# Summing a state-space scan over its 16 states by accumulating transfers instead of GpSimd adds

## The reference, cut to what matters

```python
x = x + 0.5 * ffn(layernorm(x))          # "FFN 1": 512 -> 1408 -> 512, ternary weights, sigmoid gate
x = x + ssm(layernorm(x))                # the scan
x = x + 0.5 * ffn(layernorm(x))          # "FFN 2", same weights
```

```python
dt = softplus(dt_raw @ W_dt.T + b_dt)    # per token and channel
h[n] = exp(dt * a[n]) * h[n] + dt * b[n] * xln        # over the tokens, for n = 0..15
y = sum over n of h[n] * c[n]
out = y + xln * D_param
```

## Time and profile before

| | us |
|---|---|
| median of 3 runs (lowest, highest) | 925.68 (922.63, 927.62) |
| profiled execution, first to last instruction | 922.9 |
| one chunk, second to seventh | 98.0 to 98.9 |
| DVE busy | 817.9 (89%) |
| PE busy | 681.0 (74%) |
| POOL busy | 591.3 (64%) |
| ACT busy | 566.3 (61%) |

### The profile page before, as it was taken

One profiled execution on the slowest core, in us unless ns is written; L12 is line 12 of the kernel. 1 busy time (PEld: TensorE's weight loads), 2 busy tenths in 40 slices (PEclk: granted clock), 3 DMA queues, 4 the chain that ended last, 5 costly groups with the idle time before them and its releaser, 6 DMA issues. The chain is left out here.

```text
span 922.9 us, 15428 instructions
## 1 busy us (share of the span) xinstructions
PE 681.0 (74%) x5152; PEld 555.8 (60%) x5152; DVE 817.9 (89%) x1113; ACT 566.3 (61%) x1298; POOL 591.3 (64%) x418
## 2 busy tenths in 40 slices
PE   5566595368986888688986898789769894247568
PEld 4455374157865776567764786578557773035457
DVE  4974999899998999899989998999989998989931
ACT  5413565857587667955795768765885587355232
POOL 0370274776678758866777678876887488637502
PEclk7787797669997999889997998799979998559869
DMA  9300000000001000010001000100000000000000
GB/s 365 89 1 24 0 1 23 1 0 2 1 1 47 1 1 1 10 40 1 2 1 47 1 2 1 47 1 1 1 24 1 1 1 2 23 0 1 23 1 24
DMA packets 15009, 18.82 MB, mean 20 GB/s; under 512 B 3664, under 2 KB 12368, under 8 KB 14928
## 3 DMA queue, kind: packets, MB, share of 16 engines
q1 hardware_dynamic: 14928, 17.80, 5.6%
HBM read 13.60 MB, written 4.19 MB: 19 GB/s over the span
## 5 line engine op out<-in xcount | busy, mean ns | idle before, releaser
L344 PE MATMUL work<-x_hi,q 128*128 128x256 f16 x1408 | 338.0, 286 | 38.9 <-DVE hid L831 20.3
L344 PE MATMUL work<-x_lo,q 128*128 128x256 f16 x1408 | 336.7, 285 | 0.0
L1080 POOL TENSOR_TENSOR shared<-shared 128x1024 f32<-128x1024 f32 x120 | 284.5, 2371 | 60.3 <-DVE shared L902 59.9
L892 DVE TENSOR_TENSOR_SCAN shared<-decay,last_state,shared 128x256 f32<-128x256 f32 x448 | 304.4, 729 | 13.8 <-ACT decay L689 7.3
L689 ACT ACTIVATE decay<-shared,a_neg 128x256 f32<-128x256 f32 x512 | 221.1, 468 | 111.9 <-DVE shared L892 107.4
L1064 POOL TENSOR_TENSOR hid_lo<-hid,hid_hi 128x256 f16<-128x256 f32 x176 | 122.0, 707 | 137.9 <-ACT hid_hi L626 137.1
L344 PE MATMUL work<-hid_hi,q 128*128 128x256 f16 x704 | 162.6, 279 | 38.0 <-POOL hid_lo L1064 18.5
L344 PEld LDWEIGHTS work<-x_hi,q 128*128 128x128 f16 x1408 | 144.7, 103 | 71.8 <-DVE hid L831 25.7
L344 PE MATMUL work<-hid_lo,q 128*128 128x256 f16 x704 | 162.9, 279 | 0.0
L344 PEld LDWEIGHTS work<-x_lo,q 128*128 128x128 f16 x1408 | 144.3, 102 | 23.1
L879 DVE TENSOR_TENSOR shared<-shared,bc_row 128x1024 f32<-128x1024 f32 x128 | 154.9, 1210 | 0.3
(11 more groups left out here) (112 smaller groups left out, 788.2 us busy)
## 6 DMA issues: line engine op xcount, KB each, us to landing
x_in<-xT SPq DMA_DIRECT2D x8, 512.0 KB, 4.0
outT<-x SPq DMA_DIRECT2D x7, 512.0 KB, 3.2
shared<-w1T SPq DMA_DIRECT2D x4, 704.0 KB, 7.0
shared<-w2T SPq DMA_DIRECT2D x4, 704.0 KB, 11.5
shared<-w3T SPq DMA_DIRECT2D x3, 768.0 KB, 13.5
shared<-w3T SPq DMA_DIRECT2D x1, 512.0 KB, 15.2
outT<-x SPq DMA_DIRECT2D x2, 256.0 KB, 2.2
wx<-w_xT SPq DMA_DIRECT2D x1, 256.0 KB, 11.4
```

Source lines behind the costliest of these rows:

```text
L344: return nc.tensor.matmul(out, lhsT, rhs, start=start, stop=stop)
L892: nc.vector.tensor_tensor_scan(out=states[:, n % HR, k, :], data0=decay[pair][:, j, :], data1=dbx[:, n % 2, k, :], initial=state, op0=ALU. ...
L1080: nc.gpsimd.tensor_tensor(x2[:, par, :, :] if n == NS - 1 else y[:, 0, :, :], x1d[:, par, :, :] if n == 0 else y[:, 0, :, :], prod[:, n % ...
```

## The change

The sum is made by transfers that add their source to what stands in their destination (`accum_op=ALU.add`), each issued by POOL. The products of the even states go onto `x1d`, which holds the skip path and the residual already. The product of state 1 is written by DVE straight into `y`, and those of the other odd states (3 to 15) are added onto `y`. The ring of products has four tiles instead of two. `sum_up` adds `x1d` and `y` into `x2` on POOL, in step 1 of the next chunk, and `fold_x2` moves from step 0 to step 1 with it. In the last chunk DVE makes that last add, after waiting for the transfers. POOL's chunks are written out one after another instead of in a loop over pairs of them.

```diff
 AT_POOL = dict(
-    ..., fold_x2=1, ...
+    ..., fold_x2=11, sum_up=11, ...
-        prod = carve(2)
+        prod_low = carve(2)
...
+        prod_high = sb("prod_high", [P, 2, KD, TC])
+        prod = [prod_low[:, 0], prod_low[:, 1], prod_high[:, 0], prod_high[:, 1]]
...
@@ ACT, d_times_xln (writes the skip path of chunk c)
-                    act.wait_ge(y_done, NS * (c - 2) + 1)
+                    act.wait_ge(x2_done, c - 1)
@@ DVE, times_c
-                if not (isinstance(g, int) and g < 2):
-                    dve.wait_ge(y_done, g - 1)
-                nc.vector.tensor_tensor(prod[:, n % 2, :, :], states[:, n % HR, :, :], ...
+                if n == 1:
+                    if not first(c):
+                        dve.wait_ge(x2_done, c)
+                elif n % 2 == 0 and not (isinstance(g, int) and g < 4):
+                    dve.wait_ge(even_added, 16 * (NS // 2 * c + n // 2 - 1))
+                elif n % 2 == 1 and not (isinstance(g, int) and g < 7):
+                    dve.wait_ge(odd_added, 16 * ((NS // 2 - 1) * c + max(0, n - 5) // 2))
+                nc.vector.tensor_tensor(y[:, 0, :, :] if n == 1 else prod[n % 4], states[:, n % HR, :, :], ...
@@ DVE, after the last chunk
-            dve.wait_ge(y_done, NS * NC - 1)
-            dve.wait_ge(prod_done, NS * NC)
-            nc.vector.tensor_tensor(x2[...], y[:, 0, :, :], prod[:, (NS - 1) % 2, :, :], ALU.add).then_inc(y_done, 1)
+            dve.wait_ge(even_added, 16 * (NS // 2) * NC)
+            dve.wait_ge(odd_added, 16 * (NS // 2 - 1) * NC)
+            nc.vector.tensor_tensor(x2[...], y[:, 0, :, :], x1d[:, (NC - 1) % 2, :, :], ALU.add).then_inc(x2_done, 1)
@@ POOL
-            def add_y(c, n, par):
...
-                nc.gpsimd.tensor_tensor(x2[:, par, :, :] if n == NS - 1 else y[:, 0, :, :],
-                                        x1d[:, par, :, :] if n == 0 else y[:, 0, :, :],
-                                        prod[:, n % 2, :, :], ALU.add).then_inc(y_done, 1)
+            def add_prod(c, n, par):
+
+                if n % 2 == 0:
+                    count = NS // 2 * c + n // 2
+                    if n == 0:
+                        pool.wait_ge(x1d_done, c + 1)
+                    else:
+                        pool.wait_ge(even_added, 16 * count)
+                    pool.wait_ge(prod_done, NS * c + n + 1)
+                    nc.gpsimd.dma_start(x1d[:, par, :, :], prod[n % 4], accum_op=ALU.add).then_inc(even_added, 16)
+                elif n > 1:
+                    count = (NS // 2 - 1) * c + n // 2 - 1
+                    if n > 3:
+                        pool.wait_ge(odd_added, 16 * count)
+                    pool.wait_ge(prod_done, NS * c + n + 1)
+                    nc.gpsimd.dma_start(y[:, 0, :, :], prod[n % 4], accum_op=ALU.add).then_inc(odd_added, 16)
+
+            def sum_up(c, par):
+
+                pool.wait_ge(x2_free[par], 8 * (c - par) + 16)
+                pool.wait_ge(even_added, 16 * (NS // 2) * (c + 1))
+                pool.wait_ge(odd_added, 16 * (NS // 2 - 1) * (c + 1))
+                nc.gpsimd.tensor_tensor(x2[:, par, :, :], x1d[:, par, :, :], y[:, 0, :, :], ALU.add).then_inc(x2_done, 1)
@@ POOL, beside_scan(c, par, now)
+                    if now == AT_POOL["sum_up"]:
+                        sum_up(c - 1, 1 - par)
                     if now == AT_POOL["fold_x2"]:
-                        pool.wait_ge(y_done, NS * c)
+                        pool.wait_ge(x2_done, c)
                         fold(pool, nc.gpsimd, fold_x[2], c, square[2], x2[:, 1 - par, :, :])
@@ POOL, scan_chunk
                     if s > 0:
-                        add_y(c, s - 1, par)
+                        add_prod(c, s - 1, par)
                     elif not first(c):
-                        add_y(c - 1, NS - 1, 1 - par)
+                        add_prod(c - 1, NS - 1, 1 - par)
...
-            scan_all(pool, scan_chunk)
+            for c in range(NC):
+                scan_chunk(c, c % 2)
+            add_prod(NC - 1, NS - 1, (NC - 1) % 2)
```

More of the change, by code:

```diff
@@ L65 @@
     lo1=[10, 11, 11, 21, 30, 30, 30, 40, 40, 40, 40],
-    lo2=[70, 71, 81, 90, 101, 110, 120, 120, 121, 121, 121], fold_x2=1, fold_sq2=30, x_lo2=41, softplus=140,
+    lo2=[70, 71, 81, 90, 101, 110, 120, 120, 121, 121, 121], fold_x2=11, sum_up=11, fold_sq2=30, x_lo2=41, softplus=140,
     fold_x0=60, x_lo0=141, bc_rest=120, add_x1=91)
@@ L201, in macaron @@
         dbx_done, scan_done = sem("dbx_done"), sem("scan_done")
-        prod_done, y_done = sem("prod_done"), sem("y_done")
+        prod_done, x2_done = sem("prod_done"), sem("x2_done")
+        even_added, odd_added = sem("even_prods_added"), sem("odd_prods_added")
         state_saved = sem("state_saved")
@@ L899, in times_c @@
                 dve.wait_ge(bc_done, g + 3)
-                if not (isinstance(g, int) and g < 2):
-                    dve.wait_ge(y_done, g - 1)
-                nc.vector.tensor_tensor(prod[:, n % 2, :, :], states[:, n % HR, :, :], bcast(bc_row[(n + 1) % 2][:, 1, :]),
+                if n == 1:
[5 more added lines that the diff above has]
+                    dve.wait_ge(odd_added, 16 * ((NS // 2 - 1) * c + max(0, n - 5) // 2))
+                nc.vector.tensor_tensor(y[:, 0, :, :] if n == 1 else prod[n % 4], states[:, n % HR, :, :], bcast(bc_row[(n + 1) % 2][:, 1, :]),
                                         ALU.mult).then_inc(prod_done, 1)
@@ L1034, in _ @@
             dve.wait_ge(x2_free[(NC - 1) % 2], 8 * (NC - 2) + 16)
-            dve.wait_ge(y_done, NS * NC - 1)
-            dve.wait_ge(prod_done, NS * NC)
-            nc.vector.tensor_tensor(x2[:, (NC - 1) % 2, :, :], y[:, 0, :, :], prod[:, (NS - 1) % 2, :, :], ALU.add).then_inc(y_done, 1)
-            dve.wait_ge(y_done, NS * NC)
+            dve.wait_ge(even_added, 16 * (NS // 2) * NC)
+            dve.wait_ge(odd_added, 16 * (NS // 2 - 1) * NC)
+            nc.vector.tensor_tensor(x2[:, (NC - 1) % 2, :, :], y[:, 0, :, :], x1d[:, (NC - 1) % 2, :, :], ALU.add).then_inc(x2_done, 1)
+            dve.wait_ge(x2_done, NC)
             fold(dve, nc.vector, fold_x[2], NC, square[2], x2[:, (NC - 1) % 2, :, :])
```

## The result

The changed kernel takes 968.87 us, median of 4 runs (968.05 to 969.12), against 926.33 us before in the same setting (922.63 to 927.62): a ratio of 1.0465, 95% interval 1.0443 to 1.0488. It is slower by some 43 us; the forecast was 954, range 941 to 983. The profiled execution spans 966.9 us, 44.0 more than the 922.9 before. An execution more than 1.5% slower than the fastest of its kernel is left out of medians, ratios and ranges, and named where there was one.

The account below looks back on a forecast made before the run. DVE was taken to bound the scan, with 4.3 us idle in a chunk. Six seams 20.4, last seam 2.5 and tail 5 made 27.9 us, added to the median of 925.7: 953.6, said as 954, range 941 to 983.

Parts of the forecast that it names:

- POOL does not appear as a releaser; I take zero: In the scan: DVE waits for none of the adds taken from POOL, so removing them gains 0 us.
- G: Time for which issuing one transfer holds POOL: 1.3 us, between 0.37 and 2.36.
- L: Time from a transfer's issue to its landing: 5 us, from 3.2 to 9.6; hidden in the steps below 12.3.
- the tail: Hand-over after the last chunk: DVE waits for the last product's transfer to land, plus 5 us (3.2 to 9.6).
- The seam: Between chunks, 1 to 6: later `mean2` delays blocks 3 to 6 and so DVE, 3.4 us each, 20.4 in all.
- The last seam: Start of the last chunk, without FFN 1 blocks: later `mean2` delays `centre2` by 2.5 us (1.6 to 3.6).
- little is won back: Rest of chunks 1 to 6: DVE works 94.2 of 98.5 us and its waits move along, so the delay stays.
- POOL busy falls by some 280 us: Sign in the next profile: POOL's busy time over the whole kernel drops by some 280 us.
- The rivals of the landing: Transfer taking 9.6 us delays `sum_up` 3.2 us more in all seven seams: 55 us, 981; chance 0.18.
- a step-bound transfer: In the scan's steps: from 12.3 us landing each sum is slower than the scan; at 15 about 1105; chance 0.06.
- the two without a loss in the seam: Seam delay swallowed by DVE's idle time, 929, chance 0.05; or POOL the hidden bound, so faster, 915, chance 0.05.

Follow-up runs that it names:

- The hybrid: Against the changed kernel: twelve products a chunk stay transfers, products 13 to 15 and the sums' joining are adds, seam as before; 925.18 us, ratio 1.0010 to the kernel before.
- the clock held: Changed kernel plus 56 matmuls with overwritten results, run by TensorE while it waits for the fold in each seam; 955.84 us.
- the plain copies: Changed kernel with every adding transfer turned into a plain copy, the sums left out of the computation; 962.95 us, a single execution.
- the adds: Changed kernel with each adding transfer replaced by a POOL add of the same tiles, order, ring and seam kept; 971.15 us.

## Why the prediction was right, and where its size was off

- **"POOL does not appear as a releaser; I take zero" for the removed adds: right.** The hybrid frees 142 us of POOL for a ratio of 1.001.
- **G, 1.3 us: right as the sum used it, by luck in its parts.** From the end of product 0 (307.41 + 1.20 = 308.61) to the start of `sum_up` at 309.77 pass 1.16 us, and `sum_up` itself takes 2.64 instead of 2.36, so the fold ends 5.94 us after the product (314.55) where I had 5.87. But I had made the issue begin 0.05 us after the product and hold POOL for 1.3 us. It begins 0.56 us after the product (309.17) and lets the next instruction start 0.60 us later; the two errors cancel.
- **L, 5 us: right for the issue to landing (4.5 to 4.8 medians), too small for the tail.** There 1.27 us pass between product and issue, instead of 0.56 in the seam, and DVE waits 5.96; why this issue begins later is open. The term is 5.8 instead of 5, inside its bounds of 3.2 to 9.6. In the seams landing was free, as said.
- **The seam, 3.4 us: the mechanism right, the term mis-sized: 5.1 in the chunk followed.** At block 3 DVE waits 2.18 us instead of about 1. The step that failed is block 3 starting 0.51 us after `mean2` "as before" and taking 1.90 us. It started 0.98 us after `mean2` and took 3.04 us (315.68 to 318.72). I had made PE wait 6.4 us and then let it work at the speed of the kernel before. It came back at a granted clock of 0.50 and 0.21 us a matmul. The last chunk's own row, `mean2` at 1.19 us after an idle time of 3.02 us, I had priced "at the lower clock" two paragraphs on, without asking whether the longer stand in chunks 1 to 6 would bring the same. With the clock held the seam measures 3.44 us and the total falls by 13.0. The 3.4 fits better than the waits that I had listed for it: with the clock held they are 1.10 and 0.20 us at blocks 3 and 4 as forecast, but 0.99 and 0.20 at blocks 5 and 6 instead of 2 us at block 6, and 0.49 at `centre2`.
- **The last seam, 2.5 us: right.** `centre2` starts 8.48 us after product 0 did (829.25, 837.73) instead of 5.94.
- **"little is won back": right, a little more is lost.** Seen over six chunks a chunk is 104.46 us long instead of 98.51 (I had said 102), so 5.95 more, of which the seam followed is 5.1.
- **"POOL busy falls by some 280 us": wrong, by my own terms.** With the G of 1.3 us that I used, 120 issues would have held POOL for 156 us and left 128 of the fall. It fell by 178. Nothing in the time hung on it.

The account of the 44.0 us between the two profiled executions: DVE's extra waits in six seams, 31.2 us (4.2 to 6.1 each, the waits at `centre2` and at blocks 3 to 6, none of which were there before); in the last seam 2.3; the hand-over 5.8; a wait of 1.97 us for block 0 in one chunk; DVE's busy time 3.6. That is 44.9, and 0.6 is given back in the tail, where PE's up pass took 22.94 us instead of 23.52. Why DVE is busy 3.6 us longer is open; the kernel with adds in place of transfers has it too (821.5), and the hybrid, with 96 transfers and the seam as before, does not (818.4), so it goes with the new order and not with the transfers.

The forecast of slower at 0.90 and the range of 941 to 983 held, the point was 15 us low, nearly all of it the clock (13.0 by experiment, 0.6 of it from the last seam on, where I had priced it) and the tail (0.8). The rivals of the landing and of a step-bound transfer fell by the plain copies and the adds, the two without a loss in the seam by the result itself.

## What to carry to other kernels

Work taken off an engine that nothing waits for brings nothing, whatever its share of busy time: ask first which wait of the bounding engine names it. When a hand-over between engines moves by some microseconds, look at what stands behind the waiting instruction in each engine's fixed order, for in six of the seven seams it was mostly the FFN blocks behind the late mean that cost; and if TensorE is the one that stands, price what follows at both of its clock levels. Before taking work off an engine, test the structure with the old operation in the new order, as the adds did here: that one run tells the order's price from the operation's.

## What the runs showed of the hardware

- **Idle TensorE comes back slow.** After 6.81 us of standing the next matmuls came every 0.21 us for about 3 us at a granted clock of 0.50, then every 0.11; with 56 filler matmuls in the gap and a rest of 0.93 us, every 0.11 from the start at 1.00, and the fp32 `mean2` took 0.70 instead of 1.19 us.
- **An adding transfer issued by GpSimd**, 512 KB within SBUF, has a row of 0.87 us on POOL and lands after 4.5 to 4.8 us (medians by line), a plain copy 0.57 and 2.9 us. The Trainium skill ("DMA: Bandwidth & Descriptors", Anatomy of one DMA) gives 2.0 us plus bytes over 436 GB/s, by estimate 3.2 us for this size; the copy is 0.3 us below that. "Collectives: The Full Stack" (The bandwidth ceiling) says that an adding transfer reads two sources; the 1.7 us more for adding is above the 1.2 us that a second read at that rate would take by estimate. The two misses are opposite, so the 4.4 us that the prediction had by these pages is only 0.1 to 0.4 us below the 4.5 to 4.8 measured.
- **The row of an issue on POOL overlaps the next.** The next POOL instruction starts 0.6 us after an adding issue began (309.17, 309.77), while the issue's row is 0.87 us long, and that next add takes 0.28 us more than usual (2.64 against 2.36). An adding issue thus costs POOL 0.9 us, its row, but part of it shows in the row behind.
- **DVE's one-input fp32 `tensor_scalar` is held up by a POOL add.** The same instruction, with the adds on POOL and with the transfers (two kernels):

```profile
L998 DVE TENSOR_SCALAR sp_t<-sp_e 128x1024 f32<-128x1024 f32 x7 | 11.2, 1604 | 0.0
```

```profile
L1008 DVE TENSOR_SCALAR sp_t<-sp_e 128x1024 f32<-128x1024 f32 x7 | 4.8, 687 | 0.0
```

In the first kernel it starts at 371.91 us while a POOL add runs from 370.37 to 372.96, and ends 0.55 us after it; the other six meet an add in the same way. The Trainium skill ("SBUF — State Buffer", Who interferes with whom) says that DVE in its two-port modes and GpSimd shut each other out for a whole instruction; these rows agree, if the instruction runs in such a mode, which no row names. Here, and only here, transfers in place of adds did make DVE quicker, by 6.4 us of busy time, which did not reach the end.
